# Forward row transform of a two-layer spectral kernel: sums and differences of the image's halves streamed through small tables, then transposed

## Chip, cores and metric

One core of one Trainium2 chip. The metric is the device time of one execution in microseconds, less is better.

## What is computed

The input x is 8 images of 64 channels, 256 x 256, fp32. Layer 0 mixes shifted pixels and channels; layer 1 is a Fourier layer on the normalised result. The part that matters:

```python
x = x + _L0_conv_ref(_gn(x), ...)          # stages before
# layer 1, v = _gn(x)
x_ft = jnp.fft.rfft2(v)                    # over h (rows) and w (columns)
top = jnp.einsum('bixy,ioxy->boxy', x_ft[:, :, :m1, :m2], w1)
bot = jnp.einsum('bixy,ioxy->boxy', x_ft[:, :, -m1:, :m2], w2)
...                                        # m1 = m2 = 32
x = x + jnp.fft.irfft2(out_ft, s=(h, w))   # stages after
```

Only 32 modes of w and 64 of h (from -32 to 31) are needed. The group norm's mean and variance are taken from sums of squares and folded into the modes as scales.

## The kernel before

The program is a sequence of blocks, at whose ends all engines meet: statistics of x, mixing (layer 0, which writes its result to a scratch in HBM), **the forward transform**, mixing of modes, inverse transform. The change touches the forward block alone.

The forward block goes over B = 8 batches (images), each in NG = 8 tiles of CG = 8 channels. A tile is `XW[t % 4]`, 128 partitions x 2 x 8 x 256: rows h of one half of the image on the partitions, both halves beside each other. SP loads it with two DMAs of 1 MB as soon as the tile four before it is read by TensorE (`row_done`) and by ScalarE (`sq_done`).

- **TensorE, rows (L818).** `rows(c, n)` handles four channels. For each channel and each half of the columns it multiplies the tile (128 x 128, as the weights) by the table `frow` (128 x 128 streamed: cosines and sines of 33 frequencies), once for each half of the image, and adds both in PSUM. What comes out has w on the partitions, since the tile was the weights. It alternates between PSUM banks 0-1 and 2-3.
- **VectorE (L1024)** copies 128 x 544 of each such pair of banks into `A[c % 2]`, where the channel is the innermost index: the writes step 64 elements.
- **TensorE, columns (L852).** `columns(c, m)`, m = 0 to 4, multiplies `A` of the batch by `fcol`, for 17 pairs of modes, four matmuls each; parts 0 to 3 have four pairs, part 4 has one. It uses banks 4 to 7. They run one batch later, between the rows of the next: part 0 behind rows 0, part 1 behind rows 1, and so on at every second call. `norm` (L830) is one small matmul that adds up the squares.
- **ScalarE** squares the tiles with a running sum for the variance (L904, four instructions a tile, two scratch buffers in turn), takes the root (L912), copies column parts 0 and 2 into `XB` with the scale (L924) and issues the three stores of the modes of a batch (L932).
- **VectorE** copies column parts 1, 3 and 4 (L1004), and makes the negated copy (L1012). `spread`, `variance` and `scales` are tiny.
- **GpSimd** has nothing in this block.

The order on each engine is written out by hand in the loops over c and n; an engine takes its instructions in that order, and only the semaphore waits tie the engines together. Each fp32 matmul shows in the trace as two MATMUL and two LDWEIGHTS records.

Other lines that the text names: L471, the matmuls of the mixing stage (64 columns of weights, 512 streamed, to PSUM partitions 0-63 and 64-127 in turn); L242, a transpose by TensorE; L383 and L374, a copy and a product on GpSimd; L565, L722 and L729, a copy and two three-operand instructions on VectorE; L266, small sums on ScalarE, each of which waits for the one before; L963, a copy of four elements from PSUM; L1257 and L1288, a copy from PSUM and an addition in the inverse stage.

Of the kernel before, what the change touches and what calls it, by code (L numbers as in the profile page):

```python
# [23 lines left out]
ACT = mybir.ActivationFunctionType  # L24
ALU = mybir.AluOpType
# [31 lines left out]
def constants():  # L57
# [31 lines left out]
    frow = np.zeros((P, 2, P))  # L89
    for half in range(2):  # L90
        a = th * np.outer(np.arange(P) + half * P, np.arange(NM))
        frow[:, half, :NM] = np.cos(a)
        frow[:, half, NM2:NM2 + NM] = np.sin(a)
# [21 lines left out]
def program(nc, x, w1m, b1m, w2m, b2m, sa1, sa2, gamma, beta, wr1, wi1, wr2, wi2, const, out):  # L115
    top = ExitStack()
    with top:
# [625 lines left out]
        with ph:  # L743
# [4 lines left out]
            NX = 4  # L748
            XW = [sb(ph, f"fwd_x{i}", [P, 2, CG, W]) for i in range(NX - KEPT)] + x1_kept
            A = [sb(ph, f"fwd_cols{i}", [P, 2, 4 * NP, C]) for i in range(2)]  # L750
            XB = sb(ph, "fwd_modes", [C, 3, KX, M2])
            junk = [sb(ph, f"fwd_junk{i}", [P, 2, 2 * W]) for i in range(2)]
# [7 lines left out]
            row_done, row_out, sq_done = sem("fwd_row"), sem("fwd_row_out"), sem("fwd_squares")  # L760
# [5 lines left out]
            RC = 4  # L766
            NR = C // RC
# [9 lines left out]
            with nc.Block() as block:  # L777
                @block.sync
                def _(sp):
                    for n in ("frow", "fcol", "both", "ident"):  # L780
                        sp.dma_start(*T[n]).then_inc(tab, 16)
                    for t in range(B * NG):
                        c, g = t // NG, t % NG * CG
                        if t >= NX:

                            sp.wait_ge(row_done, 2 * (t - NX + 1))
                            sp.wait_ge(sq_done, 4 * (t - NX + 1))
# [6 lines left out]
                def _(pe):  # L794
# [11 lines left out]
                    def rows(c, n):  # L806

                        t, c0 = c * NG + n // 2, n % 2 * RC
                        if c0 == 0:
                            pe.wait_ge(loaded[t % NX], loaded_by(t))  # L810

                        if c * NR + n >= 2:
                            pe.wait_ge(row_out, c * NR + n - 1)
                        for k in range(RC):
                            for s in range(2):
                                at = n % 2 * 1024 + k * 256 + s * P
                                for a in range(2):
                                    last = nc.tensor.matmul(psum[:, at:at + P],  # L818
                                                            XW[t % NX][:, a, c0 + k, s * P:(s + 1) * P],
                                                            frow[:, a, :], start=(a == 0), stop=(a == 1))  # L820
                        last.then_inc(row_done, 1)

# [10 lines left out]
                    def columns(c, m):  # L833

                        if m == 0:

                            pe.wait_ge(row_out, c * NR + NR)
                            if c == 0:
                                pe.wait_ge(n2, 4)
                        if m == 3:  # L840

                            pe.wait_ge(var_done, c + 1)
                        if m == 4:

                            pe.wait_ge(col_act, c * len(ON_ACT) + 1)
                        for p in range(4 * m, min(4 * m + 4, 17)):
                            pair = 2 if p < 16 else 1
                            at = (4 + m % 4) * 512 + p % 4 * P
# [9 lines left out]
                    for c in range(B):  # L858
                        for n in range(NR):
                            rows(c, n)  # L860
                            if c == 0:
                                continue
                            if n == 0:
                                norm(c - 1)
                                columns(c - 1, 0)
                            if n % 2 == 1 and n // 2 + 1 < PARTS:
                                columns(c - 1, n // 2 + 1)
# [18 lines left out]
                def col_views(m, par, first, count, sign, pos):  # L886
                    src = psum[par * C:(par + 1) * C, (4 + m % 4) * 512:(5 + m % 4) * 512] \
# [5 lines left out]
                def _(act):  # L893
                    def squares(t):

                        c = t // NG
                        act.wait_ge(loaded[t % NX], loaded_by(t))
                        if t % NG == 0 and c >= 2:
                            act.wait_ge(spread_done, c - 1)
                        for g in range(4):  # L900
                            k = 4 * t + g
                            if k >= 2:
                                act.wait_ge(sq_done, k - 1)
                            nc.scalar.activation(junk[g % 2][:, :, :],  # L904
                                                 XW[t % NX][:, :, 2 * g:2 * g + 2, :].rearrange("p a c w -> p a (c w)"),
                                                 ACT.Square,
                                                 accum_out=part[c % 2][:, k % GP:k % GP + 1]).then_inc(sq_done, 1)

# [26 lines left out]
                    for t in range(B * NG):  # L935
                        c, g = t // NG - 1, t % NG
                        squares(t)
                        if c < 0:
                            continue
                        if g == 0:  # L940
                            root(c)
                        if g == 1:
                            copies(c, 0)
                        if g == 2:
                            copies(c, 2)
                        if g == 6:
                            store(c)
# [7 lines left out]
                def _(dve):  # L955
# [14 lines left out]
                    dve.wait_ge(n2, 6)  # L970

# [43 lines left out]
                    for c in range(B):  # L1015
                        if c >= 1:
                            spread(c - 1)

                        if c >= 2:
                            dve.wait_ge(col_done, (c - 1) * PARTS)  # L1020
# [314 lines left out]
```

## Time and profile before

| | us |
|---|---|
| median of 3 runs | 2855.75 (2850.55 to 2856.43) |
| the profiled execution | 2856.01 |
| its span in the trace | 2854.3 |
| forward block, first rows to last column | 1273 to 1861 |

| engine | busy us | share of the span |
|---|---|---|
| TensorE matmul | 2229.2 | 78% |
| VectorE | 1712.9 | 60% |
| ScalarE | 1318.2 | 46% |
| GpSimd | 530.4 | 19% |

Times in the rows below are from the start of the span. Matmuls overlap: a matmul's own duration is longer than the distance to the next, so the pace is read from stretches of many. A share of the whole span is a mean over stages that have different limits; the windows show one stage at a time.

### The profile page before, as it was taken

How to read it: one execution, taken by the hardware profiler on the slowest of the kernel's cores; microseconds unless marked ns; L12 is line 12 of the kernel's file. 1: busy time of each engine (PE TensorE's matmuls, PEld its weight loads, DVE VectorE, ACT ScalarE, POOL GpSimd, SP SyncE). 2: the span in 40 equal slices, each digit the busy share in tenths (PEclk: the TensorE clock that was granted, in tenths of full speed). 3: DMA queues.
4: the chain of work that ended last, by engine and by line, in shares of the span. 5: the costliest groups of instructions: out<-in, count | busy, mean ns of one | idle time of the engine just before them, and what ended most of it. 6: DMA issues, size and time to landing. Idle time of an engine off the chain costs nothing. (4 is left out here: it accounts for less than half of the span.)

```text
span 2854.3 us, 38655 instructions
## 1 busy us (share of the span) xinstructions
PE 2229.2 (78%) x15026; PEld 1350.0 (47%) x15026; DVE 1712.9 (60%) x1672; ACT 1318.2 (46%) x1546; POOL 530.4 (19%) x411
## 2 busy tenths in 40 slices
PE   0000099999999999979999999927676989899874
PEld 0000033333333333339999999926663444444442
DVE  8999889999999999962333333310002545445442
ACT  1111279888988988855555444400002222221220
POOL 1000123553563464310000000000000111111112
PEclk9999999999999999989999999968898999999997
DMA  9999869999999999967777766489999999999999
GB/s 400 431 432 421 313 222 343 340 346 342 353 344 335 346 347 334 344 253 282 265 266 266 260 257 257 142 296 362 370 390 285 412 403 400 406 388 411 410 380 393
DMA packets 470459, 966.45 MB, mean 339 GB/s; under 512 B 14416, under 2 KB 391808, under 8 KB 424992
## 3 DMA queue, kind: packets, MB, share of 16 engines
q1 hardware_dynamic: 264784, 636.45, 60.3%
q10 hardware_dynamic: 169984, 192.95, 19.9%
q0 software_dynamic: 35536, 134.84, 12.1%
q8 instruction: 114, 1.87, 0.2%
q14 instruction: 41, 0.34, 0.0%
HBM read 670.59 MB, written 293.60 MB: 338 GB/s over the span
## 5 line engine op out<-in xcount | busy, mean ns | idle before, releaser
L471 PE MATMUL psum<-mix_u,wcur 128*64 128x512 f32 x2048 | 880.9, 592 | 1.3 <-DVE mix_u L565 1.3
L471 PE MATMUL psum<-mix_v,wcur 128*64 128x512 f32 x2048 | 880.9, 592 | 0.0
L471 PEld LDWEIGHTS psum<-mix_u,wcur 128*64 128x64 f32 x2048 | 277.3, 136 | 591.0 <-issue 569.8
L1193 PE MATMUL psum<-tab_irow_icol_sign,inv_t 128*128 128x512 f32 x1024 | 493.4, 606 | 10.8 <-DVE weights_or_rows L1288 10.8
L1288 DVE TENSOR_TENSOR weights_or_rows<-weights_or_rows,psum 128x1024 f32<-128x1024 f32 x224 | 273.0, 1221 | 256.2 <-PE psum L1193 232.8
L1024 DVE COPY fwd_cols<-psum 128x544 f32<-128x544 f32 x128 | 141.9, 1108 | 395.1 <-PE psum L818 395.1
L818 PE MATMUL psum<-tab_frow_fcol_both_ident,fwd_x 128*128 128x128 f32 x3072 | 352.1, 276 | 2.9 <-DMA fwd_x<-x_scratch 2.9
L383 POOL COPY mix_v<-mix_u 64x2321 f32<-64x2321 f32 x128 | 345.7, 2700 | 27.1 <-PE psum L471 19.2
L818 PEld LDWEIGHTS psum<-tab_frow_fcol_both_ident,fwd_x 128*128 128x128 f32 x3072 | 348.2, 193 | 4.2 <-DMA fwd_x<-x_scratch 3.0
L722 DVE SCALAR_TENSOR_TENSOR tiles<-psum,pcur,tiles 128x2048 f32<-128x2048 f32 x128 | 300.5, 2348 | 31.9 <-PE psum L471 31.6
L510 ACT ACTIVATE tiles<-tiles,pcur 128x2048 f32<-128x2048 f32 x128 | 268.0, 2095 | 106.7 <-DVE tiles L729 99.0
L1257 ACT ACTIVATE inv_t<-psum 128x256 f32<-128x256 f32 x256 | 98.2, 383 | 468.0 <-PE psum L1184 468.0
L287 DVE BATCH_NORM_STATS2 stats<-tiles 128x6 f32<-128x512 f32 x512 | 305.3, 679 | 13.1 <-DMA tiles<-x 12.9
L729 DVE SCALAR_TENSOR_TENSOR tiles<-tiles 128x2048 f32<-128x2048 f32 x128 | 309.7, 2419 | 4.0
L471 PEld LDWEIGHTS psum<-mix_v,wcur 128*64 128x64 f32 x2048 | 277.3, 136 | 0.0
L485 ACT ACTIVATE mix_v<-mix_u 64x2322 f32<-64x2322 f32 x128 | 273.8, 2139 | 3.1
L1193 PEld LDWEIGHTS psum<-tab_irow_icol_sign,inv_t 128*128 128x128 f32 x1024 | 198.9, 195 | 157.5 <-issue 138.5
L1168 PE MATMUL psum<-weights_or_rows,modes_or_terms 128*16 128x64 f32 x4096 | 170.0, 358 | 117.6 <-DMA modes_or_terms<-modes_in 104.7
L498 ACT ACTIVATE tiles<-mix_u,pcur 128x2048 f32<-128x2048 f32 x128 | 254.5, 1988 | 0.1
L565 DVE COPY mix_u<-mix_u 64x2321 f32<-64x2321 f32 x128 | 238.2, 1861 | 4.0
L395 PE MATMUL psum<-raw,s_ones_dmask_spread_npix 128*128 128x24 f32 x4 | 1.0, 386 | 297.6 <-PEq L210 297.6
L1184 PE MATMUL psum<-tab_irow_icol_sign,modes_or_terms 128*128 128x256 f32 x512 | 158.8, 394 | 90.8 <-ACT modes_or_terms L1251 90.8
(185 smaller groups left out, 1639.5 us busy)
## 6 DMA issues: line engine op xcount, KB each, us to landing
mix_u<-x SPq DMA_DIRECT2D x120, 1280.0 KB, 9.3
tiles<-x SPq DMA_DIRECT2D x64, 2048.0 KB, 12.4
x_scratch<-tiles ACTq DMA_DIRECT2D x128, 1024.0 KB, 9.0
weights_or_rows<-x_scratch SPq DMA_DIRECT2D x112, 1024.0 KB, 10.8
out<-weights_or_rows POOLq DMA_DIRECT2D x112, 1024.0 KB, 15.7
fwd_x<-x_scratch SPq DMA_DIRECT2D x96, 1024.0 KB, 6.8
x_tile<-x_scratch SPq DMA_DIRECT2D x46, 1024.0 KB, 8.9
weights_or_rows<-L_conv_w_real SPq DMA_DIRECT2D x8, 4096.0 KB, 31.6
```

Source lines behind the costliest of these rows:

```text
L287: last = nc.vector.bn_stats(stats[:, at:at + 6], XT[t % NX][:, q * 512:(q + 1) * 512])
L383: nc.gpsimd.tensor_copy(V[n % NV][C:P, 0:k], U[n % NU][C:P, SHIFT:SHIFT + k]).then_inc(up_done, 1)
L471: last = nc.tensor.matmul(bank(k * 4 + q, 512, C, e * C), wcur[j][:, e, m * C:(m + 1) * C], taps[e][:, r0:r0 + 2, m:m + W], start=(m == 0) ...
L485: nc.scalar.activation(V[n % NV][0:C, 0:k], U[n % NU][C:P, 0:k], ACT.Copy).then_inc(low_done, 1)
L498: nc.scalar.activation(XC[n % 4][:, :].rearrange("p (r w) -> p r w", w=W), rows_of(U[n % NU])[:, 1:SP_ + 1, 1:W + 1], ACT.Identity, bias=p ...
L510: nc.scalar.activation(G[n % 4][:, :], XC[n % 4][:, :], ACT.Sigmoid, bias=pcur[j][:, 1:2], scale=pcur[j][:, 0:1]).then_inc(sig_done, 1)
L565: nc.vector.tensor_copy(U[n % NU][C:P, 0:k], U[n % NU][0:C, SHIFT:SHIFT + k]).then_inc(doubled, 1)
L722: nc.vector.scalar_tensor_tensor(out=G[n % 4][:, :], in0=psum[:, k * SC:(k + 1) * SC], scalar=pcur[j][:, 3:4], in1=G[n % 4][:, :], op0=ALU ...
L729: nc.vector.scalar_tensor_tensor(out=G[n % 4][:, :], in0=G[n % 4][:, :], scalar=1.0, in1=XC[n % 4][:, :], op0=ALU.add, op1=ALU.mult, accum ...
L818: last = nc.tensor.matmul(psum[:, at:at + P], XW[t % NX][:, a, c0 + k, s * P:(s + 1) * P], frow[:, a, :], start=(a == 0), stop=(a == 1))
L1193: last = nc.tensor.matmul(bank(n % 2 * 2 + a), TS[n % 2][:, a * P:(a + 1) * P], icol, start=True, stop=True)
L1288: nc.vector.tensor_tensor(xw, xw, psum[:, n % 2 * 1024:n % 2 * 1024 + 1024] .rearrange("p (a k) -> p a k", a=2), ALU.add).then_inc(added, 1)
```

## The change

`frow` becomes two tables of 64 columns, one for the even frequencies and one for the odd. With E = upper half + lower half of the image and D = upper - lower, the even frequencies need E alone and the odd ones D alone. VectorE makes E and GpSimd makes D, 128 x 1024 each, four deep (`ED`). The tables are now the weights and E and D are streamed, 512 elements to a matmul; even frequencies go to PSUM partitions 0-63 and odd ones to 64-127 of one bank. What comes out has frequencies on the partitions, so each bank is copied to SBUF (`RS`, by ScalarE for even n and by VectorE for odd n), transposed by TensorE in four 128 x 128 pieces into bank 4 or 5, and copied to `A` by VectorE in two instructions (`turned`). n now counts pairs of channels; a unit u is two pairs, 16 units a batch. The columns have banks 6 and 7 only. The squares have one scratch buffer instead of two.

The diff, with context and blank lines left out and the indents narrowed:

```diff
...
-frow = np.zeros((P, 2, P))
-for half in range(2):
-  a = th * np.outer(np.arange(P) + half * P, np.arange(NM))
-  frow[:, half, :NM] = np.cos(a)
-  frow[:, half, NM2:NM2 + NM] = np.sin(a)
+frow = np.zeros((P, 2, C))
+for par in range(2):
+  k = np.arange(par, NM, 2)
+  a = th * np.outer(np.arange(P), k)
+  frow[:, par, :len(k)] = np.cos(a)
+  frow[:, par, NP:NP + len(k)] = np.sin(a)
...
-NX = 4
+NX, NE = 4, 4
...
+ED = [[sb(ph, f"fwd_{n}{i}", [P, CG // 2, W]) for n in ("sum", "diff")] for i in range(NE)]
+RS = [sb(ph, f"fwd_rows{i}", [P, 512]) for i in range(4)]
...
-junk = [sb(ph, f"fwd_junk{i}", [P, 2, 2 * W]) for i in range(2)]
+junk = [sb(ph, f"fwd_junk{i}", [P, 2, 2 * W]) for i in range(1)]
...
-row_done, row_out, sq_done = sem("fwd_row"), sem("fwd_row_out"), sem("fwd_squares")
+sq_done, sums_done, diff_done = sem("fwd_squares"), sem("fwd_sums"), sem("fwd_diff")
+row_done, row_act, row_dve = sem("fwd_row"), sem("fwd_row_act"), sem("fwd_row_dve")
+tr_done, tr_out = sem("fwd_turned"), sem("fwd_turned_out")
...
-RC = 4
-NR = C // RC
+NR = C // 2
+NU_ = B * NR // 2
...
-        sp.wait_ge(row_done, 2 * (t - NX + 1))
+        sp.wait_ge(sums_done, 2 * (t - NX + 1))
+        sp.wait_ge(diff_done, 2 * (t - NX + 1))
...
-    def rows(c, n):
-      t, c0 = c * NG + n // 2, n % 2 * RC
-      if c0 == 0:
-        pe.wait_ge(loaded[t % NX], loaded_by(t))
-      if c * NR + n >= 2:
-        pe.wait_ge(row_out, c * NR + n - 1)
-      for k in range(RC):
-        for s in range(2):
-          at = n % 2 * 1024 + k * 256 + s * P
-          for a in range(2):
-            last = nc.tensor.matmul(psum[:, at:at + P],
-                        XW[t % NX][:, a, c0 + k, s * P:(s + 1) * P],
-                        frow[:, a, :], start=(a == 0), stop=(a == 1))
+    def rows(n):
+      if n % 2 == 0:
+        pe.wait_ge(sums_done, n // 2 + 1)
+        pe.wait_ge(diff_done, n // 2 + 1)
+      if n >= 4:
+        pe.wait_ge(row_dve if n % 2 else row_act, (n - 4) // 2 + 1)
+      for par in range(2):
+        last = nc.tensor.matmul(bank(n % 4, 512, C, par * C), frow[:, par, :],
+                    ED[n // 2 % NE][par][:, n % 2 * 2:n % 2 * 2 + 2, :],
+                    start=True, stop=True)
...
+    def transposes(n):
+      pe.wait_ge(row_dve if n % 2 else row_act, n // 2 + 1)
+      if n == 0:
+        pe.wait_ge(n2, 4)
+      if n >= 2:
+        pe.wait_ge(tr_out, n - 1)
+      for q in range(4):
+        at = (4 + n % 2) * 512 + q * P
+        last = nc.tensor.transpose(psum[:, at:at + P], RS[n % 4][:, q * P:(q + 1) * P], ident)
+      last.then_inc(tr_done, 1)
...
-        pe.wait_ge(row_out, c * NR + NR)
-        if c == 0:
-          pe.wait_ge(n2, 4)
+        pe.wait_ge(tr_out, (c + 1) * NR)
+      if m == 1:
+        pe.wait_ge(var_done, c + 1)
+      if m == 2:
+        pe.wait_ge(col_act, c * len(ON_ACT) + 1)
...
-        pe.wait_ge(var_done, c + 1)
+        pe.wait_ge(col_dve, c * len(ON_DVE) + 1)
...
-        pe.wait_ge(col_act, c * len(ON_ACT) + 1)
+        pe.wait_ge(col_act, c * len(ON_ACT) + 2)
...
-        at = (4 + m % 4) * 512 + p % 4 * P
+        at = (6 + m % 2) * 512 + p % 4 * P
...
-    for c in range(B):
-      for n in range(NR):
-        rows(c, n)
-        if c == 0:
-          continue
-        if n == 0:
-          norm(c - 1)
-          columns(c - 1, 0)
-        if n % 2 == 1 and n // 2 + 1 < PARTS:
-          columns(c - 1, n // 2 + 1)
+    rows(0)
+    rows(1)
+    for u in range(NU_):
+      c, g, second = u // 16 - 1, u % 16 // 2, u % 2 == 1
+      if u + 1 < NU_:
+        rows(2 * u + 2)
+        rows(2 * u + 3)
+      transposes(2 * u)
+      transposes(2 * u + 1)
+      if c >= 0 and g == 0 and not second:
+        norm(c)
+      if c >= 0 and second and g < PARTS:
+        columns(c, g)
...
-    src = psum[par * C:(par + 1) * C, (4 + m % 4) * 512:(5 + m % 4) * 512] \
+    src = psum[par * C:(par + 1) * C, (6 + m % 2) * 512:(7 + m % 2) * 512] \
...
-    def squares(t):
+    def squares(t, half):
...
-      act.wait_ge(loaded[t % NX], loaded_by(t))
-      if t % NG == 0 and c >= 2:
-        act.wait_ge(spread_done, c - 1)
-      for g in range(4):
+      if half == 0:
+        act.wait_ge(loaded[t % NX], loaded_by(t))
+        if t % NG == 0 and c >= 2:
+          act.wait_ge(spread_done, c - 1)
+      for g in (2 * half, 2 * half + 1):
...
-        if k >= 2:
-          act.wait_ge(sq_done, k - 1)
-        nc.scalar.activation(junk[g % 2][:, :, :],
+        if k >= 1:
+          act.wait_ge(sq_done, k)
+        nc.scalar.activation(junk[0][:, :, :],
...
+    def row_copy(n):
+      act.wait_ge(row_done, n + 1)
+      if n >= 4:
+        act.wait_ge(tr_done, n - 3)
+      nc.scalar.activation(RS[n % 4][:, :], bank(n % 4), ACT.Copy).then_inc(row_act, 1)
...
-    for t in range(B * NG):
-      c, g = t // NG - 1, t % NG
-      squares(t)
+    squares(0, 0)
+    squares(0, 1)
+    for u in range(NU_):
+      c, t, second = u // 16 - 1, u // 2, u % 2 == 1
+      row_copy(2 * u)
+      if t + 1 < B * NG:
+        squares(t + 1, u % 2)
...
-      if g == 0:
+      if u % 16 == 1:
...
-      if g == 1:
+      if u % 16 == 3:
...
-      if g == 2:
+      if u % 16 == 6:
...
-      if g == 6:
+      if u % 16 == 13:
...
+    def sums_of(h):
+      t = h // 2
+      dve.wait_ge(loaded[t % NX], loaded_by(t))
+      if h >= NE:
+        dve.wait_ge(row_done, 2 * (h - NE) + 2)
+      half = slice(h % 2 * CG // 2, (h % 2 + 1) * CG // 2)
+      v.tensor_tensor(ED[h % NE][0][:, :, :], XW[t % NX][:, 0, half, :], XW[t % NX][:, 1, half, :],
+              ALU.add).then_inc(sums_done, 1)
+    def row_copy(n):
+      dve.wait_ge(row_done, n + 1)
+      if n >= 4:
+        dve.wait_ge(tr_done, n - 3)
+      v.tensor_copy(RS[n % 4][:, :], bank(n % 4)).then_inc(row_dve, 1)
+    def turned(n):
+      c, c0 = n // NR, n % NR * 2
+      if n % NR == 0 and c >= 2:
+        dve.wait_ge(col_done, (c - 1) * PARTS)
+      dve.wait_ge(tr_done, n + 1)
+      src = bank(4 + n % 2).rearrange("p (c a m) -> p c a m", c=2, a=2)
+      dst = A[c % 2][:, :, :, c0:c0 + 2].rearrange("p a m c -> p c a m")
+      for par in range(2):
+        last = v.tensor_copy(dst[:, :, :, par::2], src[:, :, :, par * C:par * C + 2 * NP])
+      last.then_inc(tr_out, 1)
...
-    for c in range(B):
-      if c >= 1:
-        spread(c - 1)
-      if c >= 2:
-        dve.wait_ge(col_done, (c - 1) * PARTS)
-      for n in range(NR):
-        c0, m = n * RC, n // 2
-        dve.wait_ge(row_done, c * NR + n + 1)
-        nc.vector.tensor_copy(
-          A[c % 2][:, :, :, c0:c0 + RC].rearrange("p a m c -> p c a m"),
-          psum[:, n % 2 * 1024:n % 2 * 1024 + 1024]
-          .rearrange("p (c a m) -> p c a m", c=RC, a=2)[:, :, :, 0:2 * NM2]).then_inc(row_out, 1)
-        if c == 0:
-          continue
-        if n == 0:
-          variance(c - 1)
-        if n == 1:
-          scales(c - 1)
-        if n % 2 == 1:
-          if m in ON_DVE:
-            copies(c - 1, m)
-          if m == PARTS:
-            finish(c - 1)
+    sums_of(0)
+    sums_of(1)
+    for u in range(NU_ + 1):
+      c, at = u // 16 - 1, u % 16
+      if u < NU_:
+        row_copy(2 * u + 1)
+        if c >= 0 and at == 0:
+          spread(c)
+      if u >= 1:
+        turned(2 * u - 2)
+        turned(2 * u - 1)
+      if u + 2 < NU_:
+        sums_of(u + 2)
+      if c < 0 or u == NU_:
+        continue
+      if at == 1:
+        variance(c)
+      if at == 2:
+        scales(c)
+      if at in (5, 8, 10):
+        copies(c, ON_DVE[(5, 8, 10).index(at)])
+      if at == 11:
+        finish(c)
...
+      @block.gpsimd
+      def _(pool):
+    for h in range(2 * B * NG):
+      t = h // 2
+      pool.wait_ge(loaded[t % NX], loaded_by(t))
+      if h >= NE:
+        pool.wait_ge(row_done, 2 * (h - NE) + 2)
+      half = slice(h % 2 * CG // 2, (h % 2 + 1) * CG // 2)
+      nc.gpsimd.tensor_tensor(ED[h % NE][1][:, :, :], XW[t % NX][:, 0, half, :],
+                  XW[t % NX][:, 1, half, :], ALU.subtract).then_inc(diff_done, 1)
...
```

## Rows read from the trace of the kernel before

**Rows 1.** The page's TensorE clock in 40 slices of the span.

```profile
PEclk9999999999999999989999999968898999999997
```

**Rows 2.** Windows: start:end, length, busy us (instructions) of each engine, PEclk, DMA share, GB/s.

```profile
1334.00:1407.00 73.00, 73.00 (x653) 72.71 (x652) 22.77 (x34) 37.17 (x73) 0.00 (x0) 1.00 0.66 237
1273.40:1334.00 60.60, 60.59 (x523) 60.59 (x524) 17.67 (x16) 39.68 (x73) 0.00 (x0) 0.96 0.86 339
1844.60:1860.50 15.90, 15.77 (x138) 15.44 (x138) 3.34 (x11) 3.47 (x9) 0.00 (x0) 1.00 0.01 1
```

**Rows 3.** Groups of lines by form, 1250 to 1880 us: count, busy us, mean ns, idle before.

```profile
L818 PE MATMUL psum<-tab_frow_fcol_both_ident,fwd_x 128*128 128x128 f32 x3072 | 352.1, 276 | 2.9 <-DMA fwd_x<-x_scratch 2.9
L818 PE MATMUL psum<-tab_frow_fcol_both_ident,x_tile 128*128 128x128 f32 x1024 | 117.0, 275 | 0.0
L852 PE MATMUL psum<-tab_frow_fcol_both_ident,fwd_cols 128*128 128x128 f32 x1024 | 119.7, 276 | 0.0
L904 ACT ACTIVATE fwd_junk<-fwd_x 128x1024 f32<-128x1024 f32 x192 | 200.0, 1043 | 35.3 <-DMA fwd_x<-x_scratch 34.8
L1024 DVE COPY fwd_cols<-psum 128x544 f32<-128x544 f32 x128 | 141.9, 1108 | 395.1 <-PE psum L818 395.1
L1004 DVE TENSOR_SCALAR fwd_modes<-psum,ncur 64x256 f32<-64x256 f32 x64 | 27.9, 476 | 12.2 <-PE psum L852 11.8
```

**Rows 4.** Waits, 1250 to 1880 us: total us, times, longest.

```profile
DVE fwd_cols L1024 <- PE psum L818: 395.1, 128, 7.8
```

**Rows 5.** Timeline of TensorE: start us, us; rows, mixing stage, a transpose.

```profile
1503.92 7.31 PE L818 MATMUL psum<-tab_frow_fcol_both_ident,fwd_x 128*128 128x128 f32 x64
...
600.05 0.59 PE L471 MATMUL psum<-mix_u,wcur 128*64 128x512 f32 x1
600.06 0.59 PE L471 MATMUL psum<-mix_v,wcur 128*64 128x512 f32 x1
600.48 0.59 PE L471 MATMUL psum<-mix_u,wcur 128*64 128x512 f32 x1
...
34.57 0.42 PE L242 MATMUL psum<-s_ones_dmask_spread_npix,w1d 128*64 128x128 f32 x1 [34.57 <-DMA b1r<-L_conv_mlp_b]
```

**Rows 6.** Timeline of VectorE and then GpSimd, mixing stage.

```profile
1222.11 1.36 DVE L565 COPY mix_u<-mix_u 64x2321 f32<-64x2321 f32 x1
1223.51 4.09 DVE L729 SCALAR_TENSOR_TENSOR tiles<-tiles 128x2048 f32<-128x2048 f32 x1
...
1222.12 3.34 POOL L383 COPY mix_v<-mix_u 64x2321 f32<-64x2321 f32 x1
```

**Rows 7.** Durations by line, ns min/median/max: GpSimd and VectorE, mixing stage.

```profile
L383 POOL COPY mix_v<-mix_u x128: 2117/2119/4159, 343.9 to 1225.9; 64x2321 f32<-64x2321 f32 x128
L374 POOL TENSOR_TENSOR mix_u<-mix_u,one x128: 227/233/2312, 339.9 to 1221.8; 128x20 f32<-128x20 f32 x128
L729 DVE SCALAR_TENSOR_TENSOR tiles<-tiles x128: 2291/2293/4094, 381.9 to 1255.6; 128x2048 f32<-128x2048 f32 x128
```

**Rows 8.** The same of four other lines.

```profile
L1257 ACT ACTIVATE inv_t<-psum x256: 383/383/385, 2176.2 to 2818.1; 128x256 f32<-128x256 f32 x128
L1288 DVE TENSOR_TENSOR weights_or_rows<-weights_or_rows,psum x224: 1202/1221/1223, 2188.5 to 2821.5; 128x1024 f32<-128x1024 f32 x112
L963 DVE COPY norm_values<-psum x2: 152/158/163, 1270.5 to 1270.6; 128x4 f32<-128x4 f32 x2
L932 ACTq DMA_DIRECT2D modes_in<-fwd_modes x24: 473/614/2709, 1393.9 to 1864.1; - x24
```

**Rows 9.** Timeline of ScalarE, statistics stage.

```profile
37.20 0.19 ACT L266 ACTIVATION_READ_ACCUMULATOR junk<-tiles  x1
37.51 0.23 ACT L266 ACTIVATE junk<-tiles 128x16 f32<-128x16 f32 x1
```

**Rows 10.** Windows of the inverse stage, columns as in Rows 2.

```profile
2300.00:2350.00 50.00, 41.09 (x111) 21.52 (x110) 22.12 (x20) 14.19 (x20) 7.05 (x8) 0.90 1.02 416
2350.00:2400.00 50.00, 50.00 (x141) 26.60 (x140) 28.68 (x24) 8.99 (x24) 7.93 (x10) 1.00 1.01 392
```

## The prediction

> **What bounds the kernel now.** I read the page's clock line, then the stage in windows, then the groups of lines in it, then the waits. The forward stage (row transforms, column transforms, stores of the modes) runs from 1273 to 1861 us. In each of the seven middle stretches of 73 us, one for each batch whose rows run beside the columns of the batch before, TensorE is busy for all 73 us at the full clock, while VectorE has 23 us, ScalarE 37, GpSimd nothing and the DMA engines 0.66 [rows 1, 2]. The first batch, with rows alone, takes 60.6 us; the last one's columns run alone for 15.9 us behind the rows. VectorE's copy out of PSUM waits 395 us for TensorE, the longest wait of the stage [rows 4]. So this stage is bound by TensorE alone, and what TensorE saves is time until another engine is full. The stages before and after are not touched: all engines meet between them.
>
> **The unit.** The new loops go in units of four channels, 16 to a batch, 128 in all. Before, a unit is one call of rows(): 32 matmul instructions (4096 in [rows 3], two to each fp32 matmul), and 64 take 7.31 us less a tail, so 113 ns each and 3.6 us a unit [rows 3, 5]. The columns are 136 instructions, 15.5 us a batch, and don't change.
>
> **TensorE after.** The rows of a unit are now four fp32 matmuls (two channel pairs, sum and difference), 64 columns of weights, 512 streamed, to the two halves of PSUM's partitions. The stage before has the same form at L471: two instructions for the two halves start 10 ns apart, the next two 0.43 us later [rows 5]. So four steps of 0.43: 1.7 us. (If the two passes of one half had to follow before the other half begins, five steps, 2.15.) Added are eight 128x128 transposes. The only fp32 transposes of the trace are single ones like L242, one instruction each [rows 5]; there is no stream of them. Lower bound half of a pass, 56 ns; upper bound two passes as for a matmul, 225 ns; I take one pass, 113 ns, since one instruction is issued and the weight load beside it is of the size that keeps to that pace at L818. That gives 0.9 us (0.45 to 1.8). A unit has 2.6 us, a batch 16 x 2.6 + 15.5 = 57.5 us against 73.
>
> **VectorE after.** It loses the copy of 128x544, 1.108 us [rows 3]. It gains, per unit: (1) one sum of 128x1024 with two SBUF inputs; L1288 is the same size, 1.22 us, and L729 at 2048 has 2.29, of which half is less than that [rows 7, 8]. (2) A 128x512 copy out of PSUM: the 128x4 copy has 0.158 us [rows 8], 508 more elements at the 1.07 us per 1024 that L729 and L1288 differ by give 0.69. (3) Four scattered copies of 136 elements instead of one of 544. The one of 544 takes 1.108 us, so (1.108 - 0.158)/540 = 1.76 ns an element, and 136 would take 0.39; at 1.04 ns it would be 0.30. Copies without a wait between overlap by about 0.1 us, so 0.8 to 1.2; I take 1.1. Together 1.2 + 0.6 + 1.1 and some 0.2 for waits that are just being met: 3.1 us. The copies of columns (9 of 0.48 us [rows 3]), the negation and the small ones add some 6 us a batch: 56 us.
>
> **ScalarE after.** Squares are 1.04 us each and now have one scratch buffer, so each waits for the accumulator read of the one before. The statistics stage shows that wait: the read starts at 37.20 and takes 0.19, the next instruction starts at 37.51, 0.12 after its end [rows 9]. A square then takes 0.95 + 0.19 + 0.12 = 1.26 instead of 1.04. Two of them, and a copy of 128x512 from PSUM: 0.383 for 256 at L1257 [rows 8] plus 256 at the 0.857 ns by which it differs from the square of 1024, 0.60. A unit has 3.1 us. The eight column copies (3.3 us) and three DMA issues (0.5 to 2.7 us each, median 0.61 [rows 8]) bring a batch to some 56 us. Queued behind the issues is the row copy for which the transposes wait; it may be late by about one unit less itself, 2.5 us, so it costs 1 us a batch at most.
>
> **GpSimd and the shared port.** GpSimd gets the differences, 128x1024, one a unit. A 2321-element copy takes 2.12 us, a TENSOR_TENSOR of 20 elements 0.23 [rows 7]. So 0.82 ns for each element read. Lower bound one read per element, 0.2 + 0.84 = 1.05 us; two inputs, each element read twice, 1.9 us; upper bound the stretched copies, 4.16. I take 2.0. Now the point that ties the two engines: at 1222.12 GpSimd's copy takes 3.34 us, since VectorE's copy began 10 ns earlier with 1.36; VectorE's L729, with two SBUF inputs, then takes 4.09 instead of 2.29: it ended 2.29 after GpSimd was done, less 0.15 [rows 6, 7]. Each waited for the whole of the other. The sum and the difference of a unit will thus not overlap: 1.2 + 2.0 = 3.2 us, and the difference is released late, when rows() of four units back is done, just as VectorE gets ready for the next sum.
> The Trainium skill (GPSIMD Engine Reference, Performance versus the Vector engine) gives 4497 ns for a two-input add of 2048 fp32, against my price from rows: half of it is an estimate of 2.25 us. By it the port would be taken for 3.45 us a unit and the stage would be about 10 us longer than by mine. No row here shows such an instruction at size.
>
> **Putting a batch together.** The columns stand in units 1, 3, 5, 7 (3.65 us each) and 9 (0.9). rows(u+2) stand behind them in TensorE's order and VectorE's next row copy waits for these rows, so VectorE can't run ahead: a pair of units there takes TensorE's 2 x 2.6 + 3.65 = 8.9 us, in which the others have 6.4 to 8.0. Four pairs: 35.6 us. In the other eight units TensorE waits for sums: the largest of 3.1 (VectorE, ScalarE) and 3.2 (the port), with handing over, 3.4 us; 27.2. With 1 us for the store 64 us against 73. The first batch takes 16 x 3.4, about 55, against 60.6. The start is later by a difference of 2.0 and a turn through copy and transposes, 3.5 us; the last units drain through copy, transposes, copy, 2.5 us. Where TensorE is not full the clock may dip; 5 us for that. Sum: 7 x 64 + 55 + 3.5 + 2.5 + 5 = 514 us, against 60.6 + 7 x 73 = 571. Less 57. The profiled execution took 2856.0 us (span 2854.3), the median is 2855.75: 2799.
>
> **What else is edited.** The third and fourth scratch are buffers in SBUF, no time. SP waits for three semaphores instead of two before it loads; a middle batch moved 237 GB/s and the first 339 [rows 2], a batch of 8 tiles of two 1 MB loads (16.8 MB) in 64 us asks for 262 and stores beside, and the inverse stage moves over 390 [rows 10]. Cover: 20 us a batch.
>
> **Rivals.**
> - *TensorE stays the bound* (17%): transposes at two passes, or rows in five steps. Then a unit has 3.5 us or more, a pair 10.7: 43 + 28 = 71 a batch, 7 x 71 + 57 + 6 = 560, time 2845. For it: no stream of transposes in the trace. Against: one instruction each. A coupled loop at 4.1 us a unit gives nearly the same.
> - *Clean overlap* (8%): units at 3.1, batch 59, first batch 50: 2755 to 2765. For: each engine has 56 to 58 of work. Against: the port, and four engines in one ring.
> - *The lower clock* (12%, the slower side). Before, TensorE never pauses here and has the full clock. After it pauses in each unit outside the column pairs, busy 2.6 of 3.4 us. The inverse stage, with TensorE busy 41.1 of 50 us, has a granted clock of 0.90, with 50.0 of 50 it has 1.00 [rows 10]; at the lower level (1.2 GHz) a unit takes 5.2 us, more than before. If a share s of the work runs there, a batch has 57.5 x (1 + s) by TensorE alone; from s = 0.27 on the batch is no shorter than 73. At s = 0.5: 86 a batch, some 2950. Against: at the lower level TensorE would be busy throughout, which in this stage went with the full clock. The Trainium skill (TensorE: Matmul & The Clock Gate, Part 4: PE-mode transpose) says that transposes do not hold the full clock as matmuls do; by that rule only the rows, 1.7 of 3.4 us, would speak for the full clock there, and this rival would be the likely one. The trace has no stretch of transposes to weigh it by.
> - *No change* (4%): a load or port wait of about 4.4 us a unit eats it all.
> The remaining 59% is the forecast, by itself 2775 to 2830.
>
> **Numbers.** Time 2799. Range 2758 to 2855: from clean overlap to TensorE staying the bound; left out are the lower clock and half of no change. Faster by over 0.2% (6 us, what a measurement of this kernel tells from no change): 83%; within it 5%; slower 12%.
>
> **What would show it.** L818's 4096 instructions become 1024 in pairs 0.43 us apart, 1024 transposes at 0.11; TensorE falls to about 57 of 64 us a batch; VectorE and ScalarE rise to near 55; GpSimd shows 128 instructions, some stretched beyond 2 us by the sums, and sums stretched beyond 1.22. The prediction is wrong if the transposes stand 0.22 apart, if the granted clock of the stage is below 0.9, if GpSimd's difference exceeds 3 us, or if the scattered copies cost more than 0.39 us each.

## Result: 0.8% faster, 23 us where 57 were forecast

| | median us | runs |
|---|---|---|
| before | 2853.15 | 4, 2849.77 to 2856.43 |
| changed | 2830.66 | 4, 2826.21 to 2832.58 |

The ratio is 0.9919, 95% interval 0.9900 to 0.9938. The direction was right and the time, 2831, lies in the range, but the gain is less than half of the forecast.

The page of the changed kernel, TensorE's clock first, to be held against [rows 1]; it dips in the same places as before, and a tenth deeper in two slices behind this block. Tenths of 71 us slices hide what the windows below show:

```profile
PEclk9999999999999999989999999968888999999987
```

The windows of the first batch and of two middle ones; before they are in [rows 2]. The first window here ends at the first `norm`, where the rows of the second batch have already begun:

```profile
1279.30:1339.60 60.30, 53.94 (x281) 23.83 (x282) 59.82 (x100) 51.23 (x92) 60.30 (x19) 0.97 0.92 366
1479.64:1550.74 71.10, 64.99 (x396) 37.88 (x395) 62.27 (x113) 47.92 (x90) 42.31 (x17) 0.95 0.74 270
1550.74:1619.61 68.87, 63.27 (x396) 37.85 (x395) 61.98 (x113) 47.92 (x90) 42.34 (x17) 0.98 0.75 271
```

TensorE is now busy 65 of 71.1 us and 63 of 68.9; the 1.7 us between the two go with the granted clock, 0.95 and 0.98. The `norm` matmul stands once in each batch at the same place, and so gives the length of a batch:

```profile
1339.60 0.28 PE L845 MATMUL psum<-fwd_ones,fwd_wide 128*128 128x1 f32 x2
...
1822.68 0.35 PE L845 MATMUL psum<-fwd_ones,fwd_wide 128*128 128x1 f32 x2 [0.85 <-DVE fwd_wide L1039]
```

These are seven distances in 1822.68 - 1339.60 = 483.1 us. The first six are 71.2, 68.9, 71.1, 68.9, 71.1 and 71.4 us, 70.4 on the mean; the last one, whose last two units have no rows ahead of them, is 60.6. Before, by the same instruction at 1336.45 and 1844.66, they were 508.2 us in all, six of 72.9 and a last one of 70.8. So the seven give back 25.1 us, and the first `norm` stands 3.2 us later. I had forecast 64 for each of the seven. By the starts of its row matmuls the first batch has 53.1 us, against 59.5 before and 55 forecast. Below, "a batch" is the mean of the first six distances.

The groups of the stage that answer to [rows 3], and the new ones:

```profile
L821 PE MATMUL psum<-fwd_sum,tab_frow_fcol_both_ident 128*64 128x512 f32 x512 | 262.4, 637 | 28.3 <-DVE fwd_sum L1011 28.3
L835 PE MATMUL psum<-tab_frow_fcol_both_ident,fwd_rows 128*128 128x128 f32 x1024 | 141.6, 281 | 22.8 <-DVE fwd_cols L1031 22.8
L869 PE MATMUL psum<-tab_frow_fcol_both_ident,fwd_cols 128*128 128x128 f32 x1024 | 119.2, 275 | 0.0
L1031 DVE COPY fwd_cols<-psum 128x136 f32<-128x136 f32 x512 | 142.7, 395 | 0.6 <-PE psum L835 0.6
L1019 DVE COPY fwd_rows<-psum 128x512 f32<-128x512 f32 x128 | 87.3, 682 | 50.5 <-PE psum L821 49.6
L935 ACT ACTIVATE fwd_rows<-psum 128x512 f32<-128x512 f32 x128 | 76.3, 596 | 108.7 <-PE psum L821 102.8 <-PE psum L835 2.8
L1011 DVE TENSOR_TENSOR fwd_sum<-fwd_x 128x1024 f32<-128x1024 f32 x96 | 176.3, 1837 | 2.1 <-DMA fwd_x<-x_scratch 1.7
L1115 POOL TENSOR_TENSOR fwd_diff<-fwd_x 128x1024 f32<-128x1024 f32 x96 | 267.2, 2792 | 166.1 <-PE psum L821 121.2 <-DMA fwd_x<-x_scratch 44.0
L1039 DVE COPY fwd_wide<-fwd_part 128x128 f32<-128x128 f32 x8 | 12.7, 1593 | 0.0
L1073 DVE TENSOR_TENSOR fwd_modes<-fwd_modes,ncur 64x1 f32<-64x1 f32 x8 | 14.2, 1776 | 0.1
L1074 DVE TENSOR_SCALAR fwd_modes<-fwd_modes 64x2048 f32<-64x2048 f32 x8 | 9.7, 1209 | 0.0
```

The 4096 row matmul instructions of L818 have become 1024 at L821; the line shows the half that reads sums. The sum has a mean of 1837 ns and not 1220, the difference 2792 ns. Of the two it is the sum that TensorE waits for: in the first batch a unit's difference is ready 1.1 us before its row matmuls and its sum 0.05, in the middle batches, outside the column pairs, 8 to 12 us and mostly 0.05 to 1. The last three rows are work that was there before and that the change does not touch. L1039 copies 128 x 128 within SBUF and L1073 adds one element: 1593 and 1776 ns on the mean. By line (ns min/median/max), first the changed kernel, then the one before, where the same two stand at L977 and L1011:

```profile
L1039 DVE COPY fwd_wide<-fwd_part x8: 201/1791/1796, 1336.2 to 1822.3; 128x128 f32<-128x128 f32 x8
L1073 DVE TENSOR_TENSOR fwd_modes<-fwd_modes,ncur x8: 142/2319/2322, 1389.7 to 1839.7; 64x1 f32<-64x1 f32 x8
```

```profile
L977 DVE COPY fwd_wide<-fwd_part x8: 200/204/207, 1334.0 to 1844.3; 128x128 f32<-128x128 f32 x8
L1011 DVE TENSOR_TENSOR fwd_modes<-fwd_modes,ncur x8: 152/153/157, 1392.6 to 1861.6; 64x1 f32<-64x1 f32 x8
```

What such a row does to a batch shows in the timeline behind the columns (start us, us):

```profile
1458.66 6.18 POOL L1115 TENSOR_TENSOR fwd_diff<-fwd_x 128x1024 f32<-128x1024 f32 x2 [0.50 <-PE psum L821]
1459.16 2.32 DVE L1073 TENSOR_TENSOR fwd_modes<-fwd_modes,ncur 64x1 f32<-64x1 f32 x1
1461.40 1.21 DVE L1074 TENSOR_SCALAR fwd_modes<-fwd_modes 64x2048 f32<-64x2048 f32 x1
1462.54 0.67 DVE L1019 COPY fwd_rows<-psum 128x512 f32<-128x512 f32 x1
1463.14 1.08 DVE L1031 COPY fwd_cols<-psum 128x136 f32<-128x136 f32 x4
1463.89 1.58 PE L835 MATMUL psum<-tab_frow_fcol_both_ident,fwd_rows 128*128 128x128 f32 x8 [2.50 <-DVE fwd_cols L1031]
1464.07 1.86 DVE L1011 TENSOR_TENSOR fwd_sum<-x_tile 128x1024 f32<-128x1024 f32 x1
1465.98 1.11 PE L821 MATMUL psum<-fwd_sum,tab_frow_fcol_both_ident 128*64 128x512 f32 x1 [0.51 <-DVE fwd_sum L1011]
...
1466.88 1.00 PE L821 MATMUL psum<-fwd_sum,tab_frow_fcol_both_ident 128*64 128x512 f32 x1
```

VectorE is ready at 1459.16 for the addition of one element. GpSimd has the port, and VectorE gets through at 1461.48. The negated copy takes 1.21 more. Only then come the row copy and the copies of the last transposes (L1031), for whose bank TensorE waits: idle for 2.50 us. Then the sum waits once more, and the rows of the next unit begin at 1465.98, where a unit without columns in the same batch mostly has 2.89 us, from its first row matmul to that of the next unit, and this one has 6.53. The next row matmuls start 0.90 us apart instead of 0.43 to 0.48: behind the pause the clock is on its lower level, 1.2 GHz of 1.2 and 2.4 (granted 0.50 from 1464.5 to 1467.5). At 1407.33 the same happens with L1039, 1.79 us instead of 0.20; that unit has 5.63 us.

That it is GpSimd's instruction that they wait for shows in the ends. L1073 is long in six of eight batches, and each time its record ends within 0.02 us of the end of the difference under way; L1039 is long in seven of eight, and ends 0.08 to 0.09 us behind it. In the remaining cases no difference is under way, and both take what they took before.

### The profile page after: what moved, and what is told of

The parts are those of the page before. It is cut to its first block and busy times, and to the rows that moved or that the text cites. A ratio compares the mean times of both kernels' runs of the same rounds, so it can differ in the third digit from the quotient of the medians.

```text
span 2830.6 us, 36267 instructions
## 1 busy us (share of the span) xinstructions
PE 2157.9 (76%) x12978; PEld 1068.4 (38%) x12978; DVE 2026.3 (72%) x2312; ACT 1402.6 (50%) x1674; POOL 905.2 (32%) x539
## 5 line engine op out<-in xcount | busy, mean ns | idle before, releaser
L384 POOL COPY mix_v<-mix_u 64x2321 f32<-64x2321 f32 x128 | 354.8, 2772 | 29.0 <-PE psum L472 21.1
L1115 POOL TENSOR_TENSOR fwd_diff<-fwd_x 128x1024 f32<-128x1024 f32 x96 | 267.2, 2792 | 166.1 <-PE psum L821 121.2
L730 DVE SCALAR_TENSOR_TENSOR tiles<-tiles 128x2048 f32<-128x2048 f32 x128 | 316.9, 2476 | 4.0
L821 PE MATMUL psum<-fwd_sum,tab_frow_fcol_both_ident 128*64 128x512 f32 x512 | 262.4, 637 | 28.3 <-DVE fwd_sum L1011 28.3
L821 PE MATMUL psum<-fwd_diff,tab_frow_fcol_both_ident 128*64 128x512 f32 x512 | 262.7, 638 | 0.0
L1372 POOL DMA_DIRECT2D out<-weights_or_rows x112 | 98.7, 886 | 443.5 <-DVE weights_or_rows L1360 196.8
L566 DVE COPY mix_u<-mix_u 64x2321 f32<-64x2321 f32 x128 | 228.4, 1784 | 4.0
```

The lines of the kernel that those rows point to most:

```text
L384: nc.gpsimd.tensor_copy(V[n % NV][C:P, 0:k], U[n % NU][C:P, SHIFT:SHIFT + k]).then_inc(up_done, 1)
L730: nc.vector.scalar_tensor_tensor(out=G[n % 4][:, :], in0=G[n % 4][:, :], scalar=1.0, in1=XC[n % 4][:, :], op0=ALU.add, op1=ALU.mult, accum ...
L821: last = nc.tensor.matmul(bank(n % 4, 512, C, par * C), frow[:, par, :], ED[n // 2 % NE][par][:, n % 2 * 2:n % 2 * 2 + 2, :], start=True, ...
L1115: nc.gpsimd.tensor_tensor(ED[h % NE][1][:, :, :], XW[t % NX][:, 0, half, :], XW[t % NX][:, 1, half, :], ALU.subtract).then_inc(diff_done, 1)
```

## Experiments

The kernel before ran beside all of them. The edits are shown shortened; e5 to e8 start from e1.

**e1: the two small jobs of VectorE go to ScalarE.**

```diff
-# VectorE
-v.tensor_copy(wide, part ... broadcast)            # spread, L1039
-nc.vector.tensor_tensor(XB[:, 0, 0, 0:1], XB[:, 0, 0, 0:1], ncur[0:C, 1:2], ALU.add)
-nc.vector.tensor_scalar(XB[:, 2, :, :], XB[:, 1, :, :], -1.0, None, ALU.mult)
+# ScalarE, spread behind unit 15 of a batch, finish behind unit 12
+nc.scalar.activation(wide, part ... broadcast, ACT.Copy)
+nc.scalar.activation(XB[:, 0, 0, 0:1], XB[:, 0, 0, 0:1], ACT.Identity, bias=ncur[0:C, 1:2])
+nc.scalar.activation(XB[:, 2, :, :], XB[:, 1, :, :], ACT.Copy, scale=-1.0)
```

> Both small SBUF jobs of VectorE in a batch (the 128x128 spread copy, and the one-element addition with the negated copy) are done by ScalarE; the rest of the changed kernel is as it was. Port theory (each of them waits on the port for GpSimd's whole difference, and TensorE then waits for VectorE): the two slow units of a batch, 5.6 and 6.5 us, fall to the 2.9 of the others, a batch goes from 69.0 to about 62, and the time from 2831 to about 2785. Rival, VectorE is simply full (60 to 62 of 69 us busy): only the instructions' own 1.6 us a batch come back, about 2820. Rival, ScalarE's stores hold up its row copies: no gain or slower, since ScalarE gets 2.3 us more a batch.

Measured: 2788.31 us, ratio 0.9752 (0.9731 to 0.9774). A batch has 63.4 us:

```profile
1276.00:1336.40 60.40, 53.48 (x280) 23.65 (x281) 60.12 (x100) 51.34 (x95) 60.40 (x20) 0.96 0.92 368
...
1526.90:1590.20 63.30, 61.74 (x396) 37.26 (x395) 58.78 (x110) 49.57 (x93) 43.55 (x17) 1.00 0.81 301
```

The port theory is right to 3 us. (The 69.0 of the expectation is the mean of all seven distances; that mean is now 62.9.) The two slow units have 3.0 to 3.3 and 3.16 us. The instructions moved away had 1.6 us of work a batch before; 7.0 us came back, 42.9 over the seven distances, and ScalarE got 2.5 us more without harm. So neither VectorE's fullness nor ScalarE's stores made the difference.

**e2 and e3: each of the two alone.**

```diff
# e2: finish as in e1 (behind unit 12 of a batch), spread stays
-nc.vector.tensor_tensor(XB[:, 0, 0, 0:1], ...); nc.vector.tensor_scalar(XB[:, 2, :, :], ...)
+nc.scalar.activation(XB[:, 0, 0, 0:1], ...); nc.scalar.activation(XB[:, 2, :, :], ...)
# e3: spread as in e1 (behind unit 15), finish stays
-v.tensor_copy(wide, ...)
+nc.scalar.activation(wide, ..., ACT.Copy)
```

> Only the one-element addition and the negated copy are moved to ScalarE. Port theory: the 6.5 us unit and the low clock behind it go, the 5.6 us one stays; 4.5 us a batch, about 2800. VectorE full: 1.4 us a batch, about 2821. Stores: 2831 or more.

> Only the 128x128 spread copy is moved to ScalarE. Port theory: the 5.6 us unit goes, 2.7 us a batch, about 2812. VectorE full: 0.2 us a batch, 2830. Stores: 2831.

Measured: e2 2808.43 us, ratio 0.9830 (0.9803 to 0.9856); e3 2807.30, ratio 0.9827 (0.9807 to 0.9847). A batch has 66.6 us in e2 and 66.7 in e3. Both parts are real. Their sizes are more alike than I had said (22 and 23 us, forecast 31 and 19); together they make 42. I had put the lower clock down to the 6.5 us unit alone. But in four of seven batches of the changed kernel the pause at L1039 also stretches the unit with the first column part, behind it, from 6.47 to 8.1 us. In e3 that is gone and in e2 it stays, in every second batch. And in e2 the last unit of a batch has 3.7 to 4.1 us, where the changed kernel has 2.89.

**e4: GpSimd holds the port for half as long.**

```diff
+n = CG // 2 if h < NE else CG // 4
-nc.gpsimd.tensor_tensor(ED[h % NE][1][:, :, :], ...)
+nc.gpsimd.tensor_tensor(ED[h % NE][1][:, 0:n, :], ...)      # both inputs [:, 0:n, :] too
```

> From the fifth difference on GpSimd makes only half of each (512 of 1024 elements; the other half of the buffer keeps old values), so that the port is held about half as long; everything else as in the changed kernel. Port theory: the first batch's units go from 3.32 to TensorE's 2.9 us (6 us in all), sums stay near 1.2 us, the small instructions wait half as long; about 2831 - 6 - 7 x 3 = 2804. VectorE full: the same 2831 less a few us. If a unit of 2.9 us is TensorE's own, units in the column pairs stay at 9.36 a pair.

Measured: 2769.21 us, ratio 0.9685 (0.9661 to 0.9709), with the small instructions still on VectorE. I had expected 2804: I had priced half of the small jobs' wait, but both slow units are gone (5.63 and 6.52 us have become 3.01 and 2.9), and the lower clock behind them with it. The batches are 61.56 us, all six within 0.03, with TensorE never idle:

```profile
1395.20:1456.70 61.50, 61.50 (x396) 37.28 (x395) 49.85 (x113) 46.91 (x90) 23.02 (x17) 1.00 0.84 308
```

This is TensorE's floor for this form, and it is above my 57.5. The small instructions shrink more than by half. L1073 now finds the port free in all eight batches; L1039 still meets a difference in seven, and takes 0.70 to 0.87 us. The sum's mean is near its own 1.2 us. By line group:

```profile
L1116 POOL TENSOR_TENSOR fwd_diff<-fwd_x 128x512 f32<-128x512 f32 x92 | 135.1, 1469 | 204.7 <-PE psum L821 196.5 <-DMA fwd_x<-x_scratch 8.1
L1011 DVE TENSOR_TENSOR fwd_sum<-fwd_x 128x1024 f32<-128x1024 f32 x96 | 124.5, 1297 | 3.1 <-DMA fwd_x<-x_scratch 2.6
L1039 DVE COPY fwd_wide<-fwd_part 128x128 f32<-128x128 f32 x8 | 5.4, 671 | 0.0
L1073 DVE TENSOR_TENSOR fwd_modes<-fwd_modes,ncur 64x1 f32<-64x1 f32 x8 | 1.1, 137 | 0.1
```

In the first batch units go from 3.32 to 2.89 us, as expected, after the first five. Column pairs keep 6.46 + 2.89, as in the changed kernel.

**e5: twice as many changes of form on TensorE.**

```diff
 rows(2 * u + 2)
-rows(2 * u + 3)
 transposes(2 * u)
+rows(2 * u + 3)
 transposes(2 * u + 1)
```

> On e1: TensorE's order in a unit becomes rows, transposes, rows, transposes (two matmul pairs and four transposes at a time) instead of all rows and then all transposes. The same instructions, but four changes a unit between the 64-column form and the 128-column form instead of two. Theory: the 0.26 us by which a unit (2.89) exceeds my 2.63 is the price of these two changes; then a unit takes 3.15, a column pair 9.9 instead of 9.36, a batch 2 to 4 us more, and the time is 2803 to 2820. Rival, the excess is in the semaphore waits or in the transposes themselves: then the number of changes does not matter, 2788.

Measured: 2815.05 us, ratio 0.9854 (0.9838 to 0.9870), 27 us more than e1. Two row matmul pairs and four transposes now take 1.60 us:

```profile
1503.68 0.64 PE L821 MATMUL psum<-fwd_sum,tab_frow_fcol_both_ident 128*64 128x512 f32 x1
...
1504.16 0.59 PE L821 MATMUL psum<-fwd_sum,tab_frow_fcol_both_ident 128*64 128x512 f32 x1
...
1504.69 0.66 PE L835 MATMUL psum<-tab_frow_fcol_both_ident,fwd_rows 128*128 128x128 f32 x4
...
1505.28 0.64 PE L821 MATMUL psum<-fwd_sum,tab_frow_fcol_both_ident 128*64 128x512 f32 x1
```

That is 3.19 us a unit against 2.89. The work and the number of semaphore waits are the same, so two more changes cost 0.30 us. The first step behind a change takes 0.48 us instead of 0.43, and from the last row step to the transposes there are 0.53. A batch has 67.3 us, 3.9 more than e1.

The weight loads (PEld) differ at just these places. Behind a change of form the first load begins together with its matmul; where transposes are followed by columns, the same form, it begins 0.11 us ahead:

```profile
1504.69 0.42 PEld L835 LDWEIGHTS psum<-tab_frow_fcol_both_ident,fwd_rows 128*128 128x128 f32 x4 [0.81 <-issue]
1505.28 0.13 PEld L821 LDWEIGHTS psum<-fwd_sum,tab_frow_fcol_both_ident 128*64 128x64 f32 x1 [0.17 <-issue]
...
1506.67 1.42 PEld L869 LDWEIGHTS psum<-tab_frow_fcol_both_ident,fwd_cols 128*128 128x128 f32 x12
...
1506.78 1.39 PE L869 MATMUL psum<-tab_frow_fcol_both_ident,fwd_cols 128*128 128x128 f32 x11
```

A load takes 0.13 to 0.14 us, a change 0.15. That the load which isn't hidden is the price fits, but no run tests it.

**e6: no GpSimd, VectorE makes both.**

```diff
+v.tensor_tensor(ED[h % NE][1], XW[...][:, 0, half, :], XW[...][:, 1, half, :], ALU.subtract)
-@block.gpsimd ...
```

> On e1: VectorE makes sums and differences both, GpSimd nothing, so nothing waits for the port. Theory: VectorE's own work, 4.1 us a unit (0.6 + 1.1 + 1.2 + 1.2), becomes the bound outside the column pairs, 37.4 + 8 x 4.1 = 70 to 71 us a batch, 66 for the first: about 2844. Differences of TensorE and port waits alone: if the port were what costs most, a batch would fall to TensorE's 61.6 and the time to about 2770.

Measured: 2823.90 us, ratio 0.9890 (0.9873 to 0.9906). Nobody waits for the port, both operations take 1.22 us, and VectorE bounds all units outside the column pairs, at 3.8 us. I had said 4.1 and 70 to 71 a batch; it has 67.9:

```profile
1413.10:1481.10 68.00, 62.05 (x397) 37.84 (x396) 65.64 (x126) 49.86 (x93) 0.00 (x0) 1.00 0.78 279
```

The mechanism held and the size of VectorE's unit was off. So GpSimd is worth 36 us in e1's arrangement. The changed kernel, with GpSimd but with the small jobs on VectorE, has 2831, 7 us more than this one without GpSimd.

**e7: the sum ahead of the copies.**

```diff
 row_copy(2 * u + 1)
+sums_of(u + 2)
 turned(2 * u - 2)
 turned(2 * u - 1)
-sums_of(u + 2)
```

> On e1: in VectorE's unit the sum comes before the copies of the transposes instead of behind them, so it meets GpSimd's difference at another point. Port theory: sum and difference exclude each other whatever their order, the first batch keeps 3.32 us a unit (1.20 + 2.12), time 2788 within 8. Rival, it is the phase between the two engines that costs: units of 2.9 in the first batch, 2775. It may also be slower, where the transposes now wait for their bank behind the sum.

Measured: 2855.89 us, ratio 1.000 (0.9991 to 1.001), the whole gain gone. The first batch's units have 3.32 us in this order too, so sum and difference exclude each other wherever the sum stands. But the middle batches go to 73.4 us: transposes wait for their bank behind a sum that waits for the port. In the column pairs this adds 1.5 us (7.97 and 2.89 instead of 6.46 and 2.89; the first pair 7.38), elsewhere units have 3.0 to 5.1. I had named this case and not priced it; it is larger than all else in the order.

**e8: SP issues the stores.**

```diff
-act.dma_start(xd_part[...], XB[...])      # in store(c), ScalarE, unit 13
+sp.dma_start(xd_part[...], XB[...])       # behind the load of tile 19, 27, ...
```

> On e1: the three stores of a batch's modes are issued by SP (behind the load of tile 19, 27, ...) instead of ScalarE. In e1 the row copy of the unit behind the stores starts 5.7 us after the one before, and a unit of 3.8 us stands there against 2.9. Theory: this is the issue time of the stores in ScalarE's order; about 0.9 us a batch comes back, 63.3 to 62.4, and the time goes from 2788 to about 2782. Rival: the unit is long because of the port alone, 2788. If SP's wait for the modes holds up the loads, slower than 2788.

Measured: 2782.36 us, ratio 0.9751 (0.9732 to 0.9770). Against the kernel before this is e1's ratio, and the batches are 63.4 us, as in e1. The unit behind the stores does fall, from 3.8 to 3.32 us, but the next one then has 3.32 where e1 has 2.89: five units, from the one ahead of the stores' row copy on, have 16.4 us in both. Behind e1's slow unit the next sum was ready 0.6 us before TensorE needed it; in e8 each comes 0.06 us before. So the stores on ScalarE cost a batch nothing, and that 2782 us came out as forecast is luck. (In the two profiled executions e8's stage is 4.5 us shorter, nearly all of it in the last batch and behind it: over the last columns e1's granted clock is 0.85 there and e8's 1.00. The ratios, over all runs, don't tell the two apart.) What e1 has above 61.56 comes with GpSimd's hold, since e4 has both the stores and the small jobs where the changed kernel has them and is at the floor. e1 and e8 are the fastest versions that compute the whole.

## Why the forecast was half right

**The terms.** Measured beside forecast, in us:

| term | forecast | measured |
|---|---|---|
| TensorE, rows of a unit | 1.7 | 1.87 |
| TensorE, eight transposes | 0.9 | 1.02 |
| TensorE, a batch | 57.5 | 61.6 (e4) |
| column pair | 8.9 | 9.36 |
| one scattered copy of 136 | 0.39 | 0.395 |
| row copy, VectorE / ScalarE | 0.69 / 0.60 | 0.68 / 0.60 |
| sum alone | 1.22 | 1.20 |
| difference alone | 2.0 | 2.34 to 2.38 |
| square to square, ScalarE | 1.26 | 1.17 |
| start later | 3.5 | 3.5 |
| first batch, to the first rows of the second | 55 | 53.1 |
| a middle batch, first six | 64 | 70.4 |
| last batch, with drain and its columns alone | 64 + 2.5 + 15.9 | 83.4 |
| dips of the clock, a term of its own | 5 | in the rows above |
| the whole stage, later start included | 529.9 | 562.6 |

The start is 1279.32 against 1273.41, of which 2.4 us are the stage ahead, which ended that much later in this execution. The stage before had 587.0 us by the same cuts, so it got 24 us shorter where 57 were forecast. Six middle batches with 6.4 us each above the forecast, 39 us, are more than the whole miss; the first batch was 1.9 us shorter than forecast, and the 5 us for the clock has no row of its own.

**Right.** TensorE bounded the stage, and in the four column pairs, 37.4 us of a batch or 39 with the lower clock, it does still; the form of L471 carries over; the transposes follow each other at 109 ns (eight in 0.9, and the changes beside them); VectorE can't run ahead in the column pairs; sum and difference exclude each other. Neither the rival of the lower clock nor that of transposes at two passes came true. The granted clock of the stage is 0.97, and from 1300 to 1336, where units of 3.32 us hold 1.0 us of transposes and TensorE pauses in each, it is 1.00. Of the signs that I had named, one came up: 33 of 128 differences last over 3 us. The longest has 3.38, against 2.34 alone, so this is time spent waiting for VectorE.

**The step that failed** is this: "The copies of columns, the negation and the small ones add some 6 us a batch: 56 us." I priced them by their own durations and let the port hold up only the sum. Two of them work within SBUF, use the same port, and wait there for all that is left of a difference: 1.79 us for 0.20 in seven of eight batches, and 2.32 for 0.15 in six of eight. They stand ahead of the copies that free the transposes' bank, so TensorE waits for them too, and behind most of these pauses runs on the lower clock for a few matmuls. e1 takes them away: 7.0 us a batch, 42 us in all, and lands at 2788, where I had forecast 2799 for a kernel without these waits. The row that should have told me was in [rows 7]: L374, 20 elements on GpSimd, has a median of 233 ns and a longest of 2312. How long an instruction waits on the port has nothing to do with its own size. The direct waits are 1.6 and 2.2 us a batch; the rest of the 7.0 is what they set off in the order of VectorE and TensorE, the lower clock with it. How it divides was not measured.

The Trainium skill (SBUF — State Buffer, SBUF: two separate sides) says that the pair of ports is locked for the whole instruction and that the loser fully blocks. By this rule and L1073's two SBUF inputs the 2.32 us follow; the trace agrees. I had used the rule's case in the trace for the sum alone.

**Other sizes were off and nearly cancel.** Without the small jobs (e1) a batch has 63.4 us where I had 64. The four column pairs have 37.4 us where I had 35.6: a change between the 64-column form and the 128-column form costs TensorE 0.13 to 0.15 us, two a unit (e5), which I had at nothing. On TensorE's floor that is 4.1 us a batch (61.6 for 57.5), but outside the pairs the port is the longer bound and hides it. The other eight units have 3.25 us on the mean in e1, with 2.89 where the sum is ready early, and I had 3.4: 1.2 us less a batch, and the 1 us for the store was not needed (e8). That e1 lands near my forecast is thus partly luck.

The difference is 2.34 to 2.38 us alone where I took 2.0; the Trainium skill (GPSIMD Engine Reference, Performance versus the Vector engine) gave 2.25 as an estimate by halving its figure, and was nearer. In the first batch, where GpSimd is never idle, a unit has 3.32 us. That is less than 1.20 + 2.36, since the records show each of the two begin before the other ends, and less than my 3.4: the difference's price was too low, and 0.2 us for handing over was not needed.

**Still open.** Of the first six batches of the changed kernel two have 68.9 us and four 71.1 to 71.4. The trace shows where: in the longer ones the clock falls to its lower level behind both pauses, so the unit with the first column part has 8.1 us instead of 6.47, and a unit behind the second pause 4.3 instead of 3.7; in the shorter ones it falls behind the second pause alone. Why the first pause has this in some batches only was not tried. Nor was what exactly a change of form costs TensorE (e5).

## What to carry to other kernels

When GpSimd gets work that reads SBUF, list all of VectorE's instructions that stay within SBUF, also those of one element, and add to each GpSimd's longest instruction, about the most that it waits; then look at what stands behind them in VectorE's order. Here such small jobs cost nothing on ScalarE (e1). Shorter instructions on GpSimd may help too, but e4 halves its work along with them, and the same work in more pieces was not run. A short stretch of TensorE work in another form has a price at both ends, so it is better to do more of one form at a time.

## What the runs showed of the hardware that I had not expected

- One element added on VectorE, two SBUF inputs, takes 2.32 us while GpSimd works on 1024 elements, and 0.14 to 0.15 alone.
- A two-input GpSimd operation of fp32 takes 1.27 us for 512 elements and 2.34 for 1024, so 2.1 ns an element and 0.2 fixed.
- Going from four concurrent 64-column matmul steps to 128 x 128 transposes and back costs TensorE 0.27 to 0.30 us (e4, e5); the first weight load behind each change begins with its matmul instead of ahead of it.
- fp32 transposes of 128 x 128 are one instruction each and follow each other at 0.109 us; an fp32 matmul of this size is two instructions at 0.112.
- A copy that scatters 34 fp32 in steps of 512 bytes takes 0.395 us for 136 elements, about the rate of the copy before, 1.108 us for 544 with steps of 256.
